# A transformer decoder's second cross-attention: the order of score, maximum and value matmuls at the ends of the head groups

## The reference, cut to what matters

```python
q = (Q @ Wq + bq).reshape(B, L, H, E)     # B=4, L=S=512, H=16 heads of E=16
k = (K @ Wk + bk).reshape(B, S, H, E)
v = (V @ Wv + bv).reshape(B, S, H, E)
scores = jnp.einsum('blhe,bshe->bhls', q, k)
A = jax.nn.softmax(scale * scores, axis=-1)
out = jnp.einsum('bhls,bshd->blhd', A, v).reshape(B, L, H * E)
return out @ We + be
```

## Time and profile before

| | us |
|---|---|
| median of 3 executions | 2807.13 |
| lowest, highest | 2804.55, 2814.09 |
| the profiled execution | 2809.64 |
| its span, first to last instruction | 2807.8 |
| PE busy | 2547.3 (91%) |
| DVE busy | 1428.5 (51%) |
| ACT busy | 1091.4 (39%) |
| POOL busy | 709.6 (25%) |

### The profile page before, as it was taken

One profiled execution on the slowest core, in us unless ns is written; L12 is line 12 of the kernel. 1 busy time (PEld: TensorE's weight loads), 2 busy tenths in 40 slices (PEclk: granted clock), 3 DMA queues, 4 the chain that ended last, 5 costly groups with the idle time before them and its releaser, 6 DMA issues. The chain is left out here.

```text
span 2807.8 us, 40095 instructions
## 1 busy us (share of the span) xinstructions
PE 2547.3 (91%) x16440; PEld 1558.8 (56%) x16441; DVE 1428.5 (51%) x2083; ACT 1091.4 (39%) x1885; POOL 709.6 (25%) x388
## 2 busy tenths in 40 slices
PE   7769999999999999999949978999999998599998
PEld 4346533754365534754338845364553644488887
DVE  5557437942876357832811124554455554644442
ACT  3674335822664255532512213444344433011111
POOL 0147027810865046901820020000000000022222
PEclk8979999999999999999979987999999998699999
DMA  5551002200030003100059930010010102044453
GB/s 199 212 190 34 0 1 86 78 1 1 1 140 24 1 0 123 41 1 1 1 190 331 340 126 18 1 24 23 19 28 1 24 8 98 12 160 159 159 178 91
DMA packets 62127, 219.26 MB, mean 78 GB/s; under 512 B 12293, under 2 KB 28122, under 8 KB 45178
## 3 DMA queue, kind: packets, MB, share of 16 engines
q1 hardware_dynamic: 45802, 187.39, 18.6%
q0 software_dynamic: 9568, 18.75, 2.7%
q10 hardware_dynamic: 6576, 10.57, 1.0%
HBM read 172.50 MB, written 39.99 MB: 76 GB/s over the span
## 5 line engine op out<-in xcount | busy, mean ns | idle before, releaser
L652 PE MATMUL psum<-arena 128*128 128x256 f32 (+7 forms) x4224 | 1085.1, 408 | 68.0 <-ACT arena L1528 11.5
L652 PEld LDWEIGHTS psum<-arena 128*128 128x128 f32 (+1 forms) x4224 | 672.9, 195 | 427.4 <-issue 313.1
L2495 POOL TENSOR_TENSOR arena<-arena 128x1024 f32<-128x1024 f32 x128 | 299.5, 2367 | 95.5 <-DVE arena L1996 80.9
L1996 DVE TENSOR_TENSOR_SCAN arena<-arena,psum 128x512 f32<-128x512 f32 x256 | 290.9, 1201 | 22.4 <-PE psum L793 14.5
L793 PEld LDWEIGHTS psum<-arena 128*128 128x128 f32 x2048 | 236.6, 193 | 49.3 <-ACT arena L1558 40.3
L793 PE MATMUL psum<-arena 128*128 128x128 f32 x2048 | 249.0, 279 | 2.0 <-issue 1.9
L2535 POOL DMA_INDIRECT arena<-xn,arena x32 | 31.6, 988 | 800.8 <-DVE arena L2437 793.5
L2502 POOL TENSOR_TENSOR arena<-arena 128x1024 f32<-128x1024 f32 x32 | 76.0, 2374 | 558.6 <-ACT arena L1649 558.6
L2097 DVE SCALAR_TENSOR_TENSOR arena<-psum,arena 128x1024 f32<-128x1024 f32 x128 | 156.0, 1245 | 90.5 <-PE psum L943 90.1
L1649 ACT ACTIVATE arena<-arena 128x1024 f32<-128x1024 f32 x128 | 147.1, 1149 | 44.2 <-DVE arena L2097 42.9
L1828 ACT ACTIVATE arena<-psum 128x256 f32<-128x256 f32 x128 | 49.1, 383 | 296.3 <-PE psum L652 294.9
(11 more groups left out here) (293 smaller groups left out, 3021.9 us busy)
## 6 DMA issues: line engine op xcount, KB each, us to landing
arena<-in_W SPq DMA_DIRECT2D x46, 1024.0 KB
arena<-c_rows SPq DMA_DIRECT2D x32, 512.0 KB, 4.0
arena<-in_Wg SPq DMA_DIRECT2D x16, 1024.0 KB, 4.8
arena<-in_Wu SPq DMA_DIRECT2D x16, 1024.0 KB, 7.5
arena<-in_Wd SPq DMA_DIRECT2D x16, 1024.0 KB, 10.0
arena<-in_xT SPq DMA_DIRECT2D x8, 512.0 KB, 6.1
zs_all<-arena SPq DMA_DIRECT2D x4, 1024.0 KB, 3.9
ut_all<-arena SPq DMA_DIRECT2D x4, 1024.0 KB, 8.8
```

What stands on the lines that cost most here:

```text
L652: r = mm(dst, w, x, start=i == 0, stop=i == len(pairs) - 1)
L1996: V.tensor_tensor_scan(hs[n % 3][:, c, :], dA[n % 2][:, c, :], bank[4 + c], 0.0, ALU.mult, ALU.add)\
L2495: nc.gpsimd.tensor_tensor(h, h, c_all[:, n % CBUFS, :].unsqueeze(1).broadcast_to([P, 2, L]), ALU.mult)\
```

## The change

Three things change in the cross-attention of the second layer.

- The maxima run nine pairs ahead: step `v` is followed by the pair `v + 9`, while there is one. Pair 8 is issued alone, behind `rows_of_max(0)` and ahead of step 0. The last pair, 31, so falls to step 22, and step 23 has scores alone. DVE reduces in the same order.
- At the end of a group, `rows_of_max(g + 1)` and `flip(g - 1)` come behind value tile 0, then value tile 1, then the next group's step 0 with its pair for the maxima, then the value tiles 2 and 3. Step 1 of the next group follows.
- ACT's `drain_o(g)` stands behind the first exponential of the next group. The row tiles move to bank 2, the flips of the groups 0 and 1 to banks 7 and 5, and step 1 of the groups 2 and 3 also waits for DVE to have read them.

```diff
@@ PE
-                        w(LBM.drained, LBM.upto(("max", _max_pair(g, 7))))
+                        w(LBM.drained, LBM.upto(("max", 8 * g + 7)))
...
                     if i == 1 and g > 0:
                         w(LBO.drained, g)
+                        if g > 1:
+                            w(LBM.drained, LBM.upto(("flip", g - 2)))
...
+                def score_step(v):
+
+                    scores_less_max(v)
+                    if v + 9 < V1:
+                        scores_for_max(v + 9)
+
                 rows_of_max(0)
+                scores_for_max(8)
+                score_step(0)
                 for g in range(4):
-                    for i in range(8):
-                        scores_less_max(8 * g + i)
-                        if g < 3:
-                            scores_for_max(_max_pair(g + 1, i))
-                        elif i == 2:
+                    for i in range(1, 8):
+                        score_step(8 * g + i)
+                        if g == 3 and i == 2:
                             flip(2)
-                        elif i == 5:
+                        elif g == 3 and i == 5:
                             flip_back(0)
-                    for kc in range(NC - 1):
-                        weigh_heads(g, kc)
+                    weigh_heads(g, 0)
                     if g < 3:
                         rows_of_max(g + 1)
                     if 0 < g < 3:
                         flip(g - 1)
-                    weigh_heads(g, NC - 1)
+                    weigh_heads(g, 1)
+                    if g < 3:
+                        score_step(8 * g + 8)
+                    weigh_heads(g, 2)
+                    weigh_heads(g, 3)
@@ ACT
-                    if i == 7:
-                        drain_o(g)
+                    if v == V1 - 1 or i == 0 and g > 0:
+                        drain_o(g if v == V1 - 1 else g - 1)
@@ DVE
                 add_rows(0)
+                row_max(8)
                 for g in range(3):
                     for i in range(8):
-                        row_max(_max_pair(g + 1, i))
+                        if 8 * g + i + 9 < V1:
+                            row_max(8 * g + i + 9)
```

More of the change, by code:

```diff
@@ L33, in _cross_tiles @@
 def _cross_tiles():
-    order = [(("row", 0), (0, 1))]
-    for g in range(4):
-        for i in range(8):
-            if g < 3:
[L38 to L44, removed]
+    order = [(("row", 0), (2, 1)), (("max", 8), (0, 2))]
+    for v in range(32):
+        g, i = v // 8, v % 8
+        if v + 9 < 32:
+            order.append((("max", v + 9), (2 * ((v + 9) % 2), 2)))
+        if g == 3 and i in (2, 5):
+            order.append(((("flip", 2), (0, 1)) if i == 2 else (("back", 0), (1, 1))))
+        if i == 7 and g < 3:
+            order.append((("row", g + 1), (2, 1)))
+            if g > 0:
+                order.append((("flip", g - 1), (9 - 2 * g, 1)))
     return order + [(("flip", 3), (0, 1)), (("back", 1), (1, 1))]
-def _max_pair(g, i):
-    return 8 * g + (i ^ 1)
 FFN_AT, OUT_AT = (2, 4, 6, 4), (6, 7)
```

## The result

The changed kernel takes 2813.69 us, the kernel before 2807.40 (medians of 22 executions each, taken side by side); the ratio is **1.0021**, 95% interval 1.0013 to 1.0030, so +6.3 us. Its profiled execution has a span of 2813.1 us; that of before had 2807.8.

A forecast was written before the change was run, and what follows sets the result against it. A group was bound by 9.73 us at DVE's pace plus 4.63 at PE's. Terms 0.15 + 0.71 + 0.71 + 0.05 = 1.62 us a batch, 6.5 for four, on 2807.1 gave 2813.6 us (+0.23%), range 2802 to 2822.

The forecast's parts named there:

- What sets the pace: A group takes 9.73 us at DVE's pace plus 4.63 at PE's; changed, the next group's second step waits for the copy.
- Start of group 0: Ahead of step 0, pair 8 delays it at low clock, partly regained: +0.15 us a batch, bounds -0.3 and +0.75.
- Ends of the groups 0 and 1: Value tile 3 comes 1.14 us later and the wait for the copy lies bare: +0.71 us at each end.
- the missing pair: At group 2's end, step 23 has no pair for the maxima, so the values start 0.27 us earlier.
- the value tile: At a group's end, one value tile was taken as 2.71 / 3 = 0.90 us.
- the extra turn: At a group's end, one more change from values to scores, taken as 0.08 us.
- End of group 2 and the last group: Step 25 starts about 0.7 us later, but fewer waits for ACT give that back: +0.05 us a batch.
- The rival of the falling clock: New pauses at group ends lower the clock, 1.9 us a fall: +7.6 us once per batch, 2821.2; chance 0.20.
- The rival of the free inner step: Step 16 runs in the shadow of the value tiles around it: -4.7 us, 2802.4; chance 0.12.
- The rival of the full gain: DVE goes on 1.81 us early at three ends of four batches: -21.7 us, 2785.4; chance 0.10, partial gain beyond 0.3% included.

The follow-up runs named there:

- e4: The changed kernel with the copy of a group's output in four pieces of 128 columns; ratio 1.0074 to the kernel before.
- e5: The kernel before with the copy of a group's output in four pieces of 128 columns; ratio 1.0003.
- e1: The changed kernel with maxima still nine pairs ahead but the old group end; ratio 1.0005 to the kernel before.
- e3: The changed kernel with the flip of groups 0 and 1 moved behind value tile 3; ratio 1.0022 to the kernel before.
- e6: The changed kernel with the inner step between value tiles 2 and 3, not 1 and 2; ratio 1.0024 to the kernel before.
- e8: The changed kernel with the flip behind value tile 3 and short unread matmuls in PE's pauses; ratio 1.0015 to the kernel before.
- e9: The changed kernel with two unread matmuls of 512 columns a batch ahead of group 0; ratio 1.0008 to the kernel before.
- e7: The kernel before with four unread matmuls a batch in PE's pauses ahead of group 0; ratio 0.9951.
- e7b: e7 once more, with a second trace; ratio 0.9953 to the kernel before.
- e10: e1 with two unread matmuls of 512 columns a batch ahead of group 0; ratio 0.9960 to the kernel before.

## Why the prediction was right, point by point

The forecast was 2813.6 us and +0.23%; measured are 2813.7 and +0.21%. The mechanism held. That the number hit to 0.1 us is luck: the trace's sum is 6.9 us and not 6.5, the ends cost more and the start of group 0 less than forecast, the rest of the program gave 1.6 us back in the profiled execution, and the interval of the ratio alone is 4.8 us wide.

- *What sets the pace*: right. e4 and e5 show it: 0.19 us more of copy cost 0.19 at each end after the change and 0.00 before it.
- *Start of group 0*, +0.15 with bounds -0.3 and +0.75: measured -0.42 to +0.62, on average +0.07. The six kernels with pair 8 and unfilled pauses ahead of group 0 (after, e1, e3, e4, e6, e8) have it between -0.53 and +0.80 over their 24 batches, so both bounds were a little too narrow. The start of before itself varies by 0.4 us between its batches, which the prediction, made from batch 1 alone, did not count. When the clock returns decides it: in batch 1 of the changed kernel it fell at about 1938.4 and was back at about 1941.8 (worked out from the mean clocks of 0.87 and 0.72 below). Step 0 starts there at 1940.25, so it had 1.5 us of low clock ahead of it, where step 0 of before had 5.75. In the same way for all four batches: where the clock is back 3.9 us behind the first transposes (batches 1 and 3), the start takes 12.7 us, and where it is back after 6.5 or 6.6 us (batches 2 and 0), 13.8. The +0.07 is the average of these two cases.

```profile
1938.00:1938.50 0.50, 0.50 (x6) 0.33 (x4) 0.01 (x1) 0.00 (x0) 0.00 (x0) 0.87 0.00 0
1941.50:1942.00 0.50, 0.50 (x8) 0.21 (x4) 0.23 (x1) 0.00 (x0) 0.00 (x0) 0.72 0.00 0
```

- *Ends of the groups 0 and 1*, +0.71 each: measured +0.86 and, with the 0.27 of the missing pair added back, +0.73. **The mis-sized term is the value tile.** I took 2.71 / 3 = 0.90 for each. The trace after has a single tile ahead of the transposes at 1.00 (1965.32 to 1966.32). Behind the inner step tile 3 follows tile 2 after about 0.86, if it starts 1.13 ahead of the copy as before, at 1970.27, and tile 2 at 1969.41. So I estimate a tile at about 0.86 and the turn behind it to another kind of matmul at about 0.13; before, the three tiles are 0.86, 0.86 and 0.99, which is their 2.71. A group end has one such turn behind a value tile more now: value tile 3 is 4.95 us behind tile 0 (1965.32 to 1970.27) and was 3.74 (1962.57 to 1966.31): later by 1.21 and not 1.14. Against value tile 0 the second maximum comes 7.53 us later (1950.54 to 1958.07) where it was 6.75 (1948.65 to 1955.40): +0.78. The seven maxima behind it take 8.60 where seven took 8.51, another 0.09, which I had not seen coming. "TensorEngine Tiling (Array Packing)", section "Key Properties", of the Trainium skill has the array drain at a change of tiling mode; the 0.13 agrees with that, though no run isolates the drain. I had spread the one turn of before over three tiles (0.90 each), so the extra turn came out at 0.08 and not at 0.13.
- *End of group 2 and the last group*, -0.27 and then nearly all absorbed, +0.05 in all: measured -0.27 (inside the +0.46) and +0.34, so +0.07. Right: step 25 starts 6.72 us behind group 2's value tile 0 (1980.13 to 1986.85), before 5.52, and of these 1.20 only 0.34 are left at the last group's value tile 0; the waits for ACT give the rest back.
- *The rival of the falling clock*: its mechanism is real, and in this change's own trace it did not strike: none of four last groups, none in e6, one of four in e9, two of four in e3, three of four with the longer copy. The price was wrong. In the last group a fall cost 1.6 to 2.3 us where I had priced 1.9, but five of these six falls went on behind it and made the stretch up to the next batch's first transposes longer by another 2.0 to 2.6: 4.3 to 4.5 us in all, and +17 to +18 us for one in each batch where I had 7.6. With one fall in each batch the forecast would have been about 2831 and not 2821.2. All six lie in the last group, where PE waits for ACT several times. What tips it is open: the waits of the changed kernel there (0.72, 0.52, 0.21 and 0.52 us) went with one fall in twelve last groups (after, e6, e9), and with the first of them filled by the flip, in e3, there were two falls in four.
- *The rival of the free inner step*: refuted; step 16 to value tile 2 is 1.07 us (1968.34 to 1969.41).
- *The rival of the full gain*: refuted by DVE's hole of 2.49 us. e6 adds that the early maximum has no worth of its own.

**What stays open.** Behind nearly every batch, in the norms, the clock is low for a while (not behind batch 1 in e3 and batch 0 in e8, where the stretches are 2.66 and 2.52 us shorter than before): in the kernel before from about 2007.7 to 2014.6 behind batch 1, in e7 from about 2000.4 to 2003.9. PE's timeline there, first before, then e7:

```profile
2005.58 5.06 PE L652 MATMUL psum<-arena 128*128 128x1 f32 x32 [0.32 <-ACT arena L1698]
2010.49 3.76 PE L1076 MATMUL psum<-arena 128*128 128x128 f32 x16
```

```profile
1995.92 3.73 PE L652 MATMUL psum<-arena 128*128 128x1 f32 x32 [0.32 <-ACT arena L1703]
1999.52 2.92 PE L1076 MATMUL psum<-arena 128*128 128x128 f32 x16
```

The busy times by stretch where the clock falls and where it returns, first before, then e7:

```profile
2007.00:2008.00 1.00, 1.00 (x10) 1.00 (x9) 0.00 (x0) 0.98 (x2) 0.00 (x0) 0.87 0.00 0
2014.00:2015.00 1.00, 1.00 (x4) 0.58 (x3) 0.71 (x1) 0.00 (x0) 0.00 (x0) 0.72 0.00 0
```

```profile
2000.00:2001.00 1.00, 1.00 (x9) 1.00 (x9) 0.40 (x2) 0.00 (x0) 0.00 (x0) 0.72 0.00 0
2003.00:2004.00 1.00, 1.00 (x3) 0.43 (x2) 0.70 (x1) 0.00 (x0) 0.00 (x0) 0.57 0.06 16
```

It was the shorter spell behind the first three batches in e7, e7b and e10 and the longer one in e9. That is worth 1.7 us each. Kernels with unfilled pauses have both: the changed kernel has the shorter one behind batch 1, e1 behind the batches 1 and 2. Whether the filled pauses bring it about or only move the program to other moments was not settled.

**A version that beats both** is e7_before_pe_busy: the kernel before with four unread matmuls a batch, 0.9951 and 0.9953 in two sets of runs.

## What to carry to other kernels

Before work is moved into a gap, look at what stands right behind it in the same engine's order: step 16 was not filling an idle place, it was the cover of the wait for the copy, and taking it out made the wait bare. An early start for one item is worth nothing when the second one waits for the same thing as before; the sum has to be made for the first item that is still held. And where the clock falls behind pauses of the engine, try filling them before rearranging anything: here that gave 0.5%, of which 0.3% lies in the start of group 0 and the rest between the batches, for a reason left open; the rearrangement cost 0.2%.

## What the runs showed of the hardware

- Four ACT copies of 128 columns from PSUM, back to back, took 0.79 us in all, one of 512 columns 0.60. Each of them is recorded with 0.28 (median of 64), and four of these are 1.12, so they overlap.
- The same instructions in the same order had the granted clock fall in some batches and not in others: in the last group of e4 (wait of 0.91 us) in three of four, of e9 (0.72) in one of four, of the changed kernel and e6 (0.72 as well) in none of eight. No fall in one trace does not say that there is none in the next.
- A fall in the last group cost 4.3 to 4.5 us in five of six cases, about half of it in the group where it began.
- With the clock kept up by unread matmuls, the start of group 0 was 1.95 to 2.36 us shorter; the difference of the groups 0 and 1 in one trace had given 1.9.
